# First context prepared in the last self-attention batch but one, and earlier scores in three of four cross-attention steps

## What is computed

```python
x1 = layernorm(tgt, ln1);  q, k, v = split(x1 @ sa_wqkv)
result = tgt + merge(softmax(mask(q @ k.T) * scale) @ v) @ sa_wproj + sa_bproj
xs = layernorm(src, ln2);  k2, v2 = split(xs @ ed_wkv)
q2 = layernorm(result, ln2) @ ed_wq
result = result + merge(softmax(q2 @ k2.T * scale) @ v2) @ ed_wproj + ed_bproj
result = result + relu(layernorm(tgt, ln3) @ ff_w1 + ff_b1) @ ff_w2 + ff_b2
```

## Time and profile before

| What | us |
|---|---|
| median of three runs | 1374.16 |
| profiled execution | 1374.57 |
| its span, first to last instruction | 1371.9 |
| TensorE busy | 1308.5 (95%) |
| VectorE, ScalarE, GpSimd busy | 791.6, 662.8, 703.5 |
| score matmuls' idle before them (L1756) | 5.7, of it 5.1 until a maximum was taken |
| mean granted TensorE clock | 0.989 |

### The profile page before, as it was taken

The page is one execution under the profiler, slowest core; times in us unless marked ns, Lnnn a source line. Parts: engine busy times, 40 slices in busy tenths (PEclk is TensorE's granted clock), DMA queues, the critical chain, the costliest instruction groups (busy, mean ns, idle before and its releaser), DMA issues.

```text
span 1371.9 us, 24578 instructions
## 1 busy us (share of the span) xinstructions
PE 1308.5 (95%) x9193; PEld 1078.2 (79%) x9193; DVE 791.6 (58%) x2007; ACT 662.8 (48%) x1609; POOL 703.5 (51%) x577
## 2 busy tenths in 40 slices
PE   7999999999899999999699999999999999999997
PEld 6888888888788888887577787878777787787774
DVE  6613223232767777776655565746657575575565
ACT  5311111232756665656525556564655647455444
POOL 3232221332534555557733767575676766667661
PEclk9999999999999999999899999999999999999999
DMA  7400102115636776547278667768667577766641
GB/s 231 153 16 16 62 31 77 46 60 117 149 77 177 186 166 147 122 123 186 64 150 134 116 92 116 131 112 142 91 132 116 100 130 121 124 100 106 94 67 41
DMA packets 100401, 151.67 MB, mean 111 GB/s; under 512 B 10198, under 2 KB 63230, under 8 KB 99515
## 3 DMA queue, kind: packets, MB, share of 16 engines
q1 hardware_dynamic: 100282, 150.11, 54.3%
HBM read 66.74 MB, written 24.12 MB: 66 GB/s over the span
## 4 chain that ended last, share of the span: by engine, by line
PE 70%; POOL 12%; issue 6%; DVE 6%; ACT 2%; DMA 2%; SPq 1%; POOLq 0%; ACTq 0%; DVEq 0%
PE ps L1724 16%; PE ps L453 11%; PE ps L423 10%; PE ps L164 8%; PE ps_pair L1741 6%; PE ps L1756 6%; PE ps L1770 5%; POOL ca_partial L1583 4%; PE ps L1829 3%; POOL ca_xT L1470 3%; DMA sa_K_stack<-sa_rows 1%; PE ps L1788 1%; POOL sa_fin L1029 1%; POOL sa_rows L155 1%; POOL sa_rows L157 1%
## 5 line engine op out<-in xcount | busy, mean ns | idle before, releaser
L1661 DVE TENSOR_REDUCE ca_maxes<-ps 112x1 f32<-112x375 f32 x512 | 253.1, 541 | 96.1 <-PE ps L1756 95.2
L1583 POOL TENSOR_TENSOR ca_partial<-ca_partial,ca_probT 125x896 f32<-125x896 f32 x118 | 249.6, 2115 | 102.4 <-ACT ca_probT L1604 97.8
L1604 ACT ACTIVATE ca_probT<-ps_pair 125x448 f32<-125x448 f32 x384 | 210.5, 554 | 186.9 <-PE ps_pair L1741 185.1
L312 POOL TENSOR_TENSOR ff_hT<-ff_hrelu,ff_hT 128x512 fp32r<-128x512 f32 (+1 forms) x64 | 78.7, 1231 | 203.3 <-DVE ff_hT L394 203.3
L1756 PE MATMUL ps<-ca_k_stack,ca_q_stack 96*112 96x376 f32 x512 | 167.6, 354 | 5.7 <-DVE ca_maxes L1661 5.1
L1741 PEld LDWEIGHTS ps_pair<-ca_q_stack,ca_k_stack 98*125 98x125 f32 x768 | 131.0, 187 | 42.9 <-issue 31.9
L1741 PE MATMUL ps_pair<-ca_q_stack,ca_k_stack 98*125 98x224 f32 x768 | 155.2, 284 | 1.1 <-ACT ca_probT L1604 0.9
L423 PE MATMUL ps<-ff_w,ff_hT 128*128 128x512 f32 x672 | 155.5, 390 | 0.0
L1724 PE MATMUL ps<-ca_xT,w_a 128*128 128x376 f32 x768 | 154.8, 338 | 0.0
L1724 PE MATMUL ps<-w_b,ca_xT 128*125 128x512 f32 x576 | 150.8, 398 | 3.1 <-POOL ca_xT L1470 2.4
L423 PEld LDWEIGHTS ps<-ff_w,ff_hT 128*128 128x128 f32 x672 | 125.6, 188 | 25.8
(11 more groups left out here) (145 smaller groups left out, 2422.7 us busy)
## 6 DMA issues: line engine op xcount, KB each, us to landing
ca_k_stack<-ca_keys SPq DMA_DIRECT2D x96, 376.0 KB, 8.0
sa_Q_stack<-sa_rows SPq DMA_DIRECT2D x96, 112.0 KB, 3.6
sa_K_stack<-sa_rows SPq DMA_DIRECT2D x96, 112.0 KB, 3.8
ca_q_stack<-q_out SPq DMA_DIRECT2D x96, 112.0 KB, 9.4
ctx_tokens<-in_ctx_dram SPq DMA_DIRECT2D x14, 672.0 KB
ctx_tokens<-in_L_xattn_ff_w_dram SPq DMA_DIRECT2D x16, 512.0 KB, 5.1
q_out<-sa_yT SPq DMA_DIRECT2D x16, 448.0 KB, 3.7
wp_lo<-wp_out SPq DMA_DIRECT2D x6, 1024.0 KB, 4.8
```

Source lines behind the costliest of these rows:

```text
L312: pool.tensor_tensor(hT[:, LO, m % RING, 0:width(g)], hrelu[i % 2][:, 0:width(g)], hT[:, HI, m % RING, 0:width(g)].bitcast(F32), ALU.subtr ...
L1583: pool.tensor_tensor(total, total, half(a), ALU.add).then_inc(partial_done, 1)
L1604: act.activation(probT[u // GH][0:JT, u % GH].rearrange("p a t -> p (a t)"), ps_p[u % 2][0:JT, 0:2 * T], ACT.Exp).then_inc(exp_done, 1)
L1661: dve.tensor_reduce(maxes[:, q, j, a:a + 1], ps_s[n % 3][0:TQ, 0:JH], AX_X, ALU.max).then_inc(s_read, 1)
```

## The change

The first context's tiles are loaded in slots -31, -29 and -26, measured in slots -26 to -20 and normalised in slots -18 to -13. For that the cross-attention weights are staged in the place of the self-attention key weights (`w_b`), once its last K product is done, and rounded in slots -4 to -1. The eight T go to slots -12 to -5, keys of G 0 to slots 1 and 3, V to 6 and 7, keys of G 1 to slots 11 and 13. The last batch has a table of fills of its own, with P one slot, R one slot and Y two slots earlier. In cross attention the scores of three of four steps begin with one in each of the slots 2 to 5.

```diff
-NEXT_CONTEXT = [(-2, 6), (-1, 4), (-1, 5)]
-NEXT_MEASURED = {1: (0,), 2: (1,), 7: (2,), 9: (3,), 10: (4, 5)}
-NEXT_NORMALISED = {12: (0, 1), 13: (2,), 14: (3,), 15: (4, 5)}
+NEXT_CONTEXT = [-26, -31, -29]
+NEXT_MEASURED = {-26: (2,), -25: (3,), -24: (4,), -23: (5,), -21: (0,), -20: (1,)}
+LAST_MEASURED = 1
+NEXT_NORMALISED = {-18: (0,), -17: (1,), -16: (2,), -15: (3,), -14: (4,), -13: (5,)}
+STAGED_NEXT = -17
+NEXT_ROUNDED_AT = [-4, -3, -2, -1]
...
 EARLY = {
-    (-10, BEHIND): [("pad",)],
-    (-2, BEHIND): [turned(0, 0)],
-    (-1, BEFORE): [turned_rest(0, 0)],
...
-    (3, BEFORE): [turned_rest(0, 1), turned(1, 1), ("K", 0, 0, 0)],
-    (4, BEFORE): [turned_rest(1, 1), ("K", 0, 0, 1), turned(2, 1)],
-    (4, BEHIND): [("K_rest", 0, 0), turned_rest(2, 1)],
-    (5, BEHIND): [turned(3, 1), ("context", 1, 1)],
-    (6, BEFORE): [turned_rest(3, 1), ("queries", 0), *values_of(0)],
-    (7, BEFORE): keys_of(0, 1),
-    (9, BEHIND): [("K_rest", 0, 1)],
-    (11, BEHIND): values_of(1),
...
-    (15, BEHIND): [*keys_of(1, 0), ("statistics", 1, 4), ("statistics", 1, 5), ("K_rest", 1, 0), *keys_of(1, 1), ("K_rest", 1, 1),
-                   ("queries", 1), ("ones",), ("weights",)],
+    (-14, BEHIND): [("pad",)],
+    (-12, BEHIND): [turned(0, 0)],
+    (-11, BEFORE): [turned_rest(0, 0)],
...
+    (-5, BEHIND): [turned(3, 1)],
+    (-4, BEFORE): [turned_rest(3, 1), ("context", 1, 1)],
+    (1, BEHIND): keys_of(0, 0),
+    (2, BEHIND): [("K_rest", 0, 0)],
+    (3, BEHIND): keys_of(0, 1),
+    (4, BEHIND): [("K_rest", 0, 1)],
+    (6, BEFORE): [("queries", 0), *values_of(0)],
+    (7, BEFORE): values_of(1),
+    (11, BEHIND): keys_of(1, 0),
+    (12, BEHIND): [("K_rest", 1, 0), ("statistics", 1, 0), ("statistics", 1, 1)],
+    (13, BEHIND): [*keys_of(1, 1), ("statistics", 1, 2), ("statistics", 1, 3)],
+    (15, BEHIND): [("K_rest", 1, 1), ("statistics", 1, 4), ("statistics", 1, 5), ("queries", 1), ("ones",), ("weights",)],
 }
...
+LAST_BATCH_FILLS = {0: [("Y", -2, 1)], 1: [("Y", -2, 2)], 2: [("V", 0, 0)], 3: [("V", 0, 1)], 4: [("Y", -2, 3)], 5: [("P", -1, 0)],
+                    6: [("P", -1, 1)], 11: [("R", -1, 0)], 12: [("R", -1, 1)], 13: [("Y", -1, 0)], 14: [("Y", -1, 1)], 15: [("Y", -1, 2)]}
...
     ws_next = WeightSplitter(weight_halves(ed_wkv[:, 0:C], w["q"], HD) + weight_halves(ed_wkv[:, C:2 * C], w["k"]),
-                             next_stage, [sem(f"wn_landed{i}") for i in range(2)], sem("wn_hi"), sem("wn_lo"))
+                             [w_staged[:, half, 2 * h:2 * h + 2] for half in (HI, LO) for h in range(2)],
+                             [sem(f"wn_landed{i}") for i in range(4)], sem("wn_hi"), sem("wn_lo"))
...
         if name == "stage_next":
-            sp.wait_ge(wo_stored, 64)
-            ws_next.load(sp, 0, 2)
+            wait_psum(sp, ("K", B - 1, KT - 1))
+            ws_next.load(sp)
...
         if name == "round_next":
-            if item[1] % 2 == 0:
-                wait_psum(act, ("QK"[item[1] // 2], B - 1, KT - 1))
+            if item[1] == 0:
+                wait_psum(act, ("Q", B - 1, KT - 1))
+            if item[1] >= 2:
+                act.wait_ge(ws_next.lo_done, item[1] - 1)
...
+LATE_SCORES = (0, 0, 0, 0, 0, 2, 4, 6, 8, 10, 12, 14, 16)
+EARLY_SCORES = (0, 0, 0, 1, 2, 3, 4, 6, 8, 10, 12, 14, 16)
+SCORED = (EARLY_SCORES, LATE_SCORES, EARLY_SCORES, EARLY_SCORES)
...
-            if 0 <= s - 1 < NG and 4 <= i:
-                scores = [("score", s - 1, 2 * (i - 4) + a) for a in range(2)]
+            if 0 <= s - 1 < NG:
+                scores = [("score", s - 1, u) for u in range(SCORED[g][i], SCORED[g][i + 1])]
```

More of the change, by code:

```diff
@@ L508, in xattn_kernel @@
         }
-        w_a, w_b = (top.enter_context(nc.sbuf_tensor(f"w_{n}", [P, 2, KT, C], F32R)) for n in "ab")
+        w_a = top.enter_context(nc.sbuf_tensor("w_a", [P, 2, KT, C], F32R))
+        w_b_place = nc.sbuf_base
+        w_b = top.enter_context(nc.sbuf_tensor("w_b", [P, 2, KT, C], F32R))
+        w_staged = nc.alloc_sbuf_tensor_at("w_staged", [P, 2, KT, C], F32, offset=w_b_place)
         ctx_place = nc.sbuf_base
@@ L534, in xattn_kernel @@
         banks = Banks(plan, *([top.enter_context(nc.semaphore(f"acc_{n}{i}")) for i in range(2)] for n in ("psum", "read")))
-        sa = self_attention(nc, top, cn, at, ps, banks, [i[1:] for i in plan if i[0] == "sa"], sa_weights, ctx_tokens, ctx_landed,
+        sa = self_attention(nc, top, cn, at, ps, banks, [i[1:] for i in plan if i[0] == "sa"], sa_weights, w_staged, ctx_tokens, ctx_landed,
                             ctx_ln, ctx_in, x, x_cols, cols, mask, bproj, ed_wq, ed_wkv, ed_wproj, ff, ffn_out, res_out, q2_out,
@@ L753, in plan_self_attention @@
                 items.append(("masks", b + 1))
-        normalised = (10, 11) if b < B else (9, 9)
+        normalised = (10, 11) if b < B - 1 else (9, 10) if b < B else (9, 9)
         items += [("normalise", b - 1, t) for t in range(2) if i == normalised[t] and 0 <= b - 1 < B]
@@ L773, in plan_self_attention @@
             items.append(("load_ffn", b))
-        if n in NEXT_WEIGHTS:
-            u = NEXT_WEIGHTS.index(n)
+        left = n - 16 * B
+        if left in NEXT_ROUNDED_AT:
+            u = NEXT_ROUNDED_AT.index(left)
             items.append(("round_next", u))
             rests[n + 1].append(("keep_next", u))
[L778 to L781, removed]
+        if left in NEXT_CONTEXT:
+            items.append(("next_context", NEXT_CONTEXT.index(left)))
+        items += [("next_statistics", t) for t in NEXT_MEASURED.get(left, ())]
+        items += [("next_normalise", t) for t in NEXT_NORMALISED.get(left, ())]
         if b >= B - 1:
@@ L784, in plan_self_attention, with self_attention @@
     return items
-def self_attention(nc, top, cn, at, ps, banks, plan, w, ctx_tokens, ctx_landed, ctx_ln, ctx_in, x, x_cols, cols, mask, bproj,
+def self_attention(nc, top, cn, at, ps, banks, plan, w, w_staged, ctx_tokens, ctx_landed, ctx_ln, ctx_in, x, x_cols, cols, mask, bproj,
                    ed_wq, ed_wkv, ed_wproj, ff, ffn_out, res_out, q2_out, wp_out):
@@ L969, in sync @@
                     .then_inc(y_stored, 16)
-        if name == "keep_next" and item[1] < 2:
-            ws_next.load(sp, item[1] + 2, item[1] + 3)
         if name == "next_context":
@@ L976, in sync @@
             else:
-                sp.wait_ge(ws_next.lo_done, part + 2)
+                sp.wait_ge(wo_stored, 64)
             first = ctx_in[0].rearrange("(p t) c -> p t c", t=CTX_TILES)
@@ L1019, in gpsimd @@
             ws_next.keep_lo(pool, item[1])
-        if name == "next_statistics" and item[1] == CTX_TILES - 1:
+        if name == "next_statistics" and item[1] == LAST_MEASURED:
             ctx_ln.inverse_root(pool, 0)
@@ L1556, in gpsimd @@
         if name == "pad":
-            sa.wait(pool, "values")
+            sa.wait(pool, "values", "query_stacks", "key_stacks")
             pool.memset(xT[:, :, :, :, JH:JP].bitcast(F32), 0.0).then_inc(constants_ready, 1)
@@ L1798, in tensor @@
             b, g = G // KT, G % KT
+            if (G, a, part) == (0, 0, 0):
+                sa.wait(pe, "key_weights")
             if (g, part) == (0, 0):
@@ L1805, in tensor @@
             _, b, t, part = item
+            if (b, t, part) == (0, 0, 0):
+                sa.wait(pe, "value_weights")
             if (t, part) == (0, 0):
```

37 lines of the change are left out of this document (18 added, 19 removed).

## The result

The changed kernel takes 1377.78 us (median of 19 runs), the kernel before 1375.7 us beside it (19 runs); the ratio is 1.002, with a 95% interval of 1.0014 to 1.0027. I had forecast 1368, and a time within 0.3 us of the slow end of the range, which the rivals had made wide, doesn't bear the forecast out. The profiled execution has a span of 1375.3 us against 1371.9. TensorE's busy time is the same in sum, 1308.6 against 1308.5, so the 3.4 us are idle time of TensorE; its mean granted clock went from 0.989 to 0.983.

What follows compares the result with a forecast made beforehand. The hand-over, with TensorE idle 15.9 us at a low clock and VectorE pacing slots -9 to -3, was where time could be gained. Terms summed to -6.3 us against 1374.57, so 1368 us, range 1357 to 1378.

Steps and rivals of the forecast that it cites:

- slots -22 to -17: Last self-attention batches: statistics make VectorE 2.9 us late, query product 0 moves with its split; +2.6 us, bounds 0 and +6.
- slots -16 to -13: Behind slot -17: GpSimd has room for the normalisations, so the next 12.1 us stay as they are; 0.
- slots -12 to -10: Start of the hand-over: TensorE sets the pace and receives three transpositions of the first context; 11.3 us, +1.2.
- slots -9 to -3: Hand-over: VectorE sets the pace, loses statistics, gains rests and splits; 18.7 against 16.90 us, +1.8, lower bound -1.
- slots -2 to 3: The tail: transpositions leave, work independent of ScalarE fills it; 14.5 us against 24.76, -10.3, bounds -12.8 and -5.8.
- slots 4 to 15: Behind the tail: key halves and value products cover TensorE's waits; 24.2 against 26.08 us, -1.9, bounds -3 and 0.
- steps 1 and 2: First cross-attention steps: step 1 loses a key wait, group 1's stacks land late behind the store; 26.8 against 24.66 us, +2.2.
- step 3 and all behind: Cross attention: step 3's maxima follow a late q_stack, +2.5; steady steps save score ring waits, -4.4.
- rival 3: Slots -18 to -11: VectorE and GpSimd collide at normalisations, some four meetings of 2.6 us; 1379 us, chance 0.17.
- the signs that I named: Hand-over: TensorE over 80% busy from first transposition to output projection, VectorE over 90% in slots -12 to -5, among others.
- the upper bound of this stretch: Slots -9 to -3: three of eight rests take 3.19 us instead of 0.55 while GpSimd normalises; +8.
- the steady steps: Later cross attention: early scores remove score ring waits, mainly 0.45 us in g = 2 steps; -4.4, bounds -7 and +2.

Runs made afterwards that it cites:

- e12: Changed kernel with GpSimd's rests of the key weights behind its split of query product 0 and value-weight roundings a slot later: 1374.15 us, ratio 0.9994 to before.
- e7: Changed kernel with the four roundings of the next weights, and GpSimd's rests behind them, one slot later (slots -3 to 0): 1372.93 us, ratio 0.9985 to before.
- e5: Changed kernel with the loads of group 1's key and query stacks issued ahead of the store of the last queries: 1369.23 us, ratio 0.9962 to before.
- e11: Changed kernel with stacks ahead of the store, roundings a slot later and all scores at the old slots: 1369.97 us, ratio 0.9962 to before.
- e9: Changed kernel with stacks ahead of the store, roundings a slot later and early scores from step 4 on only: 1362.97 us, ratio 0.9911 to before.
- e4: Changed kernel with the four roundings of the next key weights six slots sooner (slots -10 to -7): 1380.0 us, ratio 1.0048 to before.
- e1: Kernel before with the new tables of scores alone, the first context's work left where it was: 1372.67 us, ratio 0.9986 to before.
- e8: Changed kernel with both edits, stacks ahead of the store (e5) and roundings a slot later (e7): 1365.86 us, ratio 0.9938 to before.

## Why the prediction was wrong

By its own steps, forecast and measured in the profiles:

| step | forecast | measured |
|---|---|---|
| slots -22 to -17 | +2.6 | +1.5 |
| slots -16 to -13 | 0 | -0.4 |
| slots -12 to -10 | +1.2 | +1.8 |
| slots -9 to -3 | +1.8 | +8.6 |
| slots -2 to 3 | -10.3 | -9.5 |
| slots 4 to 15 | -1.9 | -0.4 |
| steps 1 and 2 | +2.2 | +7.3 |
| step 3 and all behind | +2.5 - 4.4 = -1.9 | -4.2 |

The measured column adds up to +4.7; the span grew by 3.4, since this execution reached the first stretch 1.3 us sooner (598.57 against 599.90).

**Right.** That the tail gains because the T are out of it; that query product 0 in slot -17 waits for VectorE's split of R, though 1.20 us and not 2 to 3; the wait for P's bank in slot -10 (1.06 us); that step 1 gets 2 us shorter (first score to M 0: 10.43 instead of 12.21); that the stack of group 1 comes late because the store is in front; step 3 (M 1 to M 2: +2.0 for +2.5). The size of the tail (-9.5 for -10.3) is in part luck: 2.5 us of my 14.5 were ScalarE's lateness, which fell in the stretch before, and in its place stood TensorE's work at a clock of 0.91 (13.31 us where I had 12.0) and 1.96 us of idle. That the whole came out near rival 3's 1379 is luck too: it had four meetings with the normalisations in slots -18 to -11, and there was hardly a cost there. Of the signs that I named, TensorE's busy share from the first T to the output projection was 72% and not over 80 (38.11 of 52.69 us), and VectorE's in slots -9 to -3 was 78% and not over 90.

**Wrong, first: slots -9 to -3, +1.8 for +8.6.** I summed VectorE's work there and asked whether it was full. But the stretch ended on a chain across ScalarE, VectorE and TensorE (activation, cast, rest, query product), and VectorE was busy for 20.01 of 25.50 us. I had ScalarE's rounding ahead of it, priced at 2.5 us, but charged it to the next stretch, where the first query product had stood before; e12 and e7 measure it at 1.9. And I weighed the meeting of VectorE and GpSimd only for the normalisations (rival 3), not for the rests of the weights, which the change puts beside R. Rival 3 had VectorE waiting for GpSimd, but in other slots (-18 to -11 instead of -6 to -3) and for other instructions. The Trainium skill, SBUF — State Buffer, "Who interferes with whom", lists copy, cast and tensor_scalar among the operations of VectorE that can take the shared ports and block fully against GpSimd; the trace agrees for all three (0.29 to 1.99 and 4.80 us, 0.39 to 2.40, 0.54 to 4.86). I had applied only its rule for two inputs.

I had also misread the meeting on which I priced rival 3 and the upper bound of this stretch. GpSimd and VectorE in the kernel before:

```profile
669.93 2.50 POOL L1015 TENSOR_TENSOR sa_res<-sa_res,sa_bias 112x512 f32<-112x512 f32 x2
...
670.39 3.19 DVE L1470 TENSOR_TENSOR ca_xT<-ca_xT_f,ca_xT 128x375 fp32r<-128x375 f32 x1
...
674.47 2.95 POOL L105 TENSOR_SCALAR ctx_tokens<-ctx_tokens,ctx_ln_mean_var,ctx_ln_rstd 125x512 f32<-125x512 f32 x1
...
674.94 0.54 DVE L1470 TENSOR_TENSOR ca_xT<-ca_xT_f,ca_xT 128x375 fp32r<-128x375 f32 x1
```

The rest of T that took 3.19 us met two additions of a bias (669.93 to 672.43), and only its end a normalisation. The next rest lay inside a normalisation and took its usual 0.54 us; there it was GpSimd's instruction that took longer, 2.95 us instead of 2.08. In the changed kernel the normalisations, from 624.61 to 645.52, cost little: no VectorE instruction took over 0.95 us there, and the copy of 1/sum at 626.06 took 0.78 instead of 0.29.

With the rounding and the rest both out of the way (e7) the stretch takes 22.4 us (647.88 to 670.31), so 3.1 of the 8.6 were theirs. Another 2.7 are query product 0 itself (667.64 to 670.31 in e7), which stood in the tail before and for which my sum here, of VectorE's work, had no term. The remaining 2.8 stand against my +1.8. The stretch in e7, at a low clock:

```profile
647.88:670.31 22.43, 15.16 (x92) 13.09 (x90) 17.96 (x61) 17.72 (x49) 3.29 (x2) 0.64 0.64 172
```

Five of the eight transpositions and the query product stand there now, TensorE is idle for a third of the stretch, and what it does takes nearly twice as long (2.87 us for a query product that takes 1.60 at full clock). Which of the moved items would have to go to keep the clock up was not tried.

**Wrong, second: steps 1 and 2, +2.2 for +7.3.** The mechanism was the one I gave, in two sizes too small. I had the last part of q_stack land 15.8 us behind the end of the last query product; the score could start after 17.5 (714.58 to 732.09), 1.25 us of it because k_stack's three issues take 3.11 us behind the store where they took 1.86 before. And I gave the rest of step 2 at full clock, 11.0 us; it took 14.4 (to 746.5), mostly since the clock fell over the wait (0.64 from 732.1 to 740 us): six key matmuls took 2.08 us where they take 1.20. Together 5.1, which is the whole difference. I also priced the lateness as a cost to be borne. It could be had for nothing, by two items in another place (e5: 7.9 us).

**Wrong, third: the steady steps, -4.4 for -6.4 to -8.** Four steps take 81.72 us with late scores and 80.90 with early ones (means from M to M, in e11 and e9). The steps of g = 2 gain 0.61 where I had 0.45, those of g = 3 lose 0.14 where I had 0.18, but those of g = 0 gain 0.35, and there I had nothing, because I read rows of g = 2 and g = 3 alone. In such a step TensorE's wait for a partial sum of GpSimd (`ca_partial`) went from 0.63 us (at 924.85 before) to 0.27 (at 933.18 in the changed kernel), which is as much as the gain. This error was on the good side and hid part of the others. Slots 4 to 15 were off by 1.5 us the other way (-0.4 for -1.9): behind TensorE's 1.96 us of idle at the end of the tail the granted clock was 0.72 for 6.1 us.

## What to carry to other kernels

When work is moved into a stretch, follow the chain that ends the stretch, engine by engine, with everything that the change puts ahead of each of its links; a sum of busy times shows only that the stretch isn't full. List VectorE's copies, casts and scalings from SBUF that will run beside GpSimd's long tensor_tensors, whoever moved, and look up what GpSimd was really doing at the time of each slow one. When items ahead of a DMA move, look at what its queue holds in front of each transfer that someone waits for soon: a load that needs nothing new doesn't belong behind a store that waits for the last product.

## What was not expected of the hardware

- VectorE's copy of 112x256 took 0.29 us alone and 1.99 beside GpSimd's tensor_tensor of 112x1024, its cast of 128x448 took 0.39 alone and 2.40 beside one of 128x1024. In e4 the copy took 4.80 us (652.24 to 657.04) and the scaling of 112x512, 0.54 alone, took 4.86 (660.87 to 665.73), each beside two such instructions in a row (to 656.90 and to 665.46): both ended behind the second and didn't get in between. In the profile this waiting is the length of VectorE's instruction and not an idle time before it.
- The same copy kept its 0.29 us inside a tensor_scalar of GpSimd (662.00 in 661.08 to 663.16, kernel before) and took 0.78 in another (626.06, changed kernel). What decides between the two was not tested.
- A wait of TensorE of 2.1 us before the early score of step 3 made M 1 to M 2 2.4 us longer in e1, e5 and e7 and 4.0 in e8 (against e9's 19.72); in e8 it was followed by a granted clock of 0.72 over 6 us, in e5 by 1.00 (742 to 748 us).
